# One block for the main loop and the general path, and a wait of TensorE for its own update ahead of each aggregate, in a graph-attention layer with experts

## What is computed

```python
xn = layernorm(x)
h = xn @ W                                    # graph attention, 4 heads of 64
e = leaky_relu(a_src[src] + a_dst[dst], 0.2)  # edges and self loops
p = exp(e - segment_max(e, dst))
gnn = relu(segment_sum(p / segment_sum(p, dst) * h[src], dst) + bias)
q, k, v = split(xn @ w_qkv + b_qkv); k = ln(k); v = ln(v)
mix = gelu((q @ (k.T @ v / N) + xn) @ w1 + b1) @ w2 + b2 + xn
x = x + gnn + mix
xn = layernorm(x) * gamma + beta
logits = xn @ Wr + br                         # 8 experts, the best 2 are taken
out = x + sum over the two of w[e] * (gelu(xn @ W1[e] + b1[e]) @ W2[e] + b2[e])
```

## Time and profile before

| | |
|---|---|
| median of 3 runs | 2322.64 us (2322.01 to 2328.99) |
| profiled execution | 2320.06 us, span 2318.3 us |
| busy in the span | TensorE 1877.7 us (81%), VectorE 1631.3 (70%), ScalarE 939.7 (41%), GpSimd 1705.2 (74%) |
| largest groups | gathers L1385 x1563, 1484.1 us; aggregate L1955 x3136, 903.1 us; L1462 x196, 446.1 us |
| mean granted TensorE clock | 0.887 |
| DMA | 451.34 MB, 195 GB/s |

### The profile page before, as it was taken

How to read it: one execution, slowest core, us unless ns; L and a number is a source line. 1 busy time by engine, 2 the same in 40 slices (tenths; PEclk the granted TensorE clock), 3 DMA queues, 4 the chain that set the end, 5 groups by cost and what they waited for, 6 DMA issues and landing times. The chain is left out here.

```text
span 2318.3 us, 36469 instructions
## 1 busy us (share of the span) xinstructions
PE 1877.7 (81%) x9261; PEld 1440.6 (62%) x9262; DVE 1631.3 (70%) x3677; ACT 939.7 (41%) x1507; POOL 1705.2 (74%) x1860
## 2 busy tenths in 40 slices
PE   8489998777877778768887888888877788888876
PEld 6367776555666656556666666666655566666655
DVE  7578888567887778876766666677656575765664
ACT  5333333345555555544444443343323243433322
POOL 3477777777777777777777777777777777777775
PEclk9789999887887778779999999999888899999988
DMA  8766655966666666677677777687767777787775
GB/s 289 165 193 173 166 159 156 299 186 174 183 182 179 174 183 178 171 200 197 195 198 199 199 198 199 189 223 194 202 198 200 201 197 203 196 213 210 191 214 160
DMA packets 296594, 451.34 MB, mean 195 GB/s; under 512 B 87393, under 2 KB 195028, under 8 KB 295874
## 3 DMA queue, kind: packets, MB, share of 16 engines
q0 software_dynamic: 87360, 242.89, 39.6%
q1 hardware_dynamic: 200028, 195.10, 28.9%
q10 hardware_dynamic: 8998, 10.96, 1.4%
HBM read 390.81 MB, written 62.13 MB: 195 GB/s over the span
## 5 line engine op out<-in xcount | busy, mean ns | idle before, releaser
L1385 POOL DMA_INDIRECT rows_g<-node_table,src_all x1563 | 1484.1, 950 | 485.2 <-issue 478.8
L1955 PE MATMUL psB<-rows_g,pick_e 128*128 128x260 f32 x3136 | 903.1, 452 | 273.0 <-issue 245.2
L1955 PEld LDWEIGHTS psB<-rows_g,pick_e 128*128 128x128 f32 x3136 | 699.6, 229 | 435.1 <-issue 303.4
L1809 ACT ACTIVATE pick_n<-local_row 128x1024 bf16<-128x1024 bf16 x196 | 207.1, 1057 | 788.5 <-PE psA L1944 760.8
L1462 DVE TENSOR_TENSOR rows_g<-rows_g,psD 128x2048 f32<-128x2048 f32 x196 | 446.1, 2276 | 0.0
L1451 DVE TENSOR_TENSOR p_both_e<-rows_g,psD 128x64 f32<-128x64 f32 x196 | 43.4, 221 | 339.3 <-DMA rows_g<-node_table,src_all 330.8
L1437 DVE TENSOR_TENSOR pick_e<-psD,slot_all 128x1024 f32<-128x1024 f32 x196 | 236.0, 1204 | 0.0
L1805 ACT ACTIVATE local_row<-local_row,minus_id 128x1024 bf16<-128x1024 bf16 x196 | 222.6, 1136 | 22.9 <-DMA local_row<-local_dram 14.6
L1990 PE MATMUL psC<-W_f,xnT 128*128 x468 | 222.1, 597 | 6.9 <-DVE hid L1495 6.9
L2040 PEld LDWEIGHTS psD<-W_f,hidT 128*128 128x128 f32 x936 | 178.2, 191 | 73.8 <-issue 55.6
L2040 PE MATMUL psD<-W_f,hidT 128*128 x936 | 221.6, 380 | 0.0
(11 more groups left out here) (327 smaller groups left out, 2279.8 us busy)
## 6 DMA issues: line engine op xcount, KB each, us to landing
local_row<-local_dram SPq DMA_DIRECT2D x196, 256.0 KB
acc<-in_L_ffn_b_dram SPq DMA_DIRECT2D x117, 256.0 KB
rows_g<-node_table,src_all POOLq DMA_INDIRECT x1563
acc<-in_L_ffn_b_dram SPq DMA_DIRECT2D x125, 128.0 KB
xin<-sent_dram SPq DMA_DIRECT2D x117, 128.0 KB
set_dram<-xn SPq DMA_DIRECT2D x117, 128.0 KB
xnT<-xT_dram SPq DMA_DIRECT2D x96, 128.0 KB, 2.6
xT_dram<-xT POOLq DMA_DIRECT2D x49, 128.0 KB, 5.7
```

The lines of the kernel that those rows point to most:

```text
L1385: pool.indirect_dma_start(out=rows_g[:, r, j], out_offset=None, in_=node_table, in_offset=bass.IndirectOffsetOnAxis(ap=src_all[:, g, j:j + ...
L1809: act.activation(pick_n[:], local_row[:, r], ACT.Relu, bias=1.0, scale=-1.0).then_inc(pick_n_ready, 1)
L1955: last = pe.matmul(ps_sum[s % 2][:, 0:AW], pick_e[:, s % SLOTS, j], rows_g[:, s % RING, j, 0:AW], start=(j == 0), stop=(j == EG - 1))
```

## The change

The diff is long because the loop's code moves one level out, into a function `loop_stage` that returns one function per engine. Leaving out white space, this is all of it:

```diff
+NEAR = 6
+    for t in final_at:
+        if final_at[t] == max(final_at.values()):
+            sum_at[t] = max(job_at) + 3
 # first phase
-            raw_at = {15: 0, 17: 1, 30: 2, 32: 3, 36: 4, 43: 5}
-            rows_weighed = {20: (0, 1), 37: (2, 3, 4), 44: (5,), 47: (6,)}
+            raw_at = {15: 0, 17: 1, 26: 2, 30: 3, 36: 4, 42: 5}
+            rows_weighed = {20: (0, 1), 31: (2, 3), 37: (4,), 43: (5,), 47: (6,)}
-                    act.dma_start(W_ext[:, :, 0:D], gnn_W.rearrange("(k p) n -> p k n", p=P)).then_inc(att_in, 16)
                     for w, a in enumerate((att_src, att_dst)):
                         act.dma_start(att_row[:, w * D:(w + 1) * D], a.rearrange("h c -> (h c)").unsqueeze(0)).then_inc(att_row_in, 16)
+                    act.dma_start(W_ext[:, :, 0:D], gnn_W.rearrange("(k p) n -> p k n", p=P)).then_inc(att_in, 16)
+                        dve.tensor_scalar(low[:], first_i[0:1, NG - WINDOWS:NG], float(P * (NT - NEAR)), None, ALU.is_lt).then_inc(beyond_ready, 1)
-                        dve.wait_ge(beyond_ready, 2)
+                        dve.wait_ge(beyond_ready, 3)
+                        dve.tensor_reduce(late_two[:, 2:3], low[:], AX_X, ALU.max).then_inc(beyond_ready, 1)
 # SyncE ahead of the loop
-                        local_rows(0)
+                    for s in range(AHEAD):
+                        local_rows(s)
                         sp.wait_ge(no_rows_set, 1)
-                        sp.dma_start(factor_dram[NT * P:], window[:, WINDOWS - 1]).then_inc(factors_out, 16)
+                    sp.dma_start(factor_dram[NT * P:], window[:, WINDOWS - 1]).then_inc(near_out, 16)
                         sp.wait_ge(parts_ready, 1)
-                        sp.dma_start(factor_dram[0:NT * P].rearrange("(t p) k c -> p t k c", p=P), factor_parts).then_inc(factors_out, 16)
-                        sp.wait_ge(factors_out, 32)
+                    sp.dma_start(factor_rows[:, NT - NEAR:], factor_parts[:, NT - NEAR:]).then_inc(near_out, 16)
+                    sp.wait_ge(near_out, 32)
                         for s in range(STEPS + LAG):
-                            if 1 <= s < NG:
+                        if AHEAD <= s < NG:
                                 local_rows(s)
+                        if s == WINDOWS:
+                            sp.wait_ge(far_out, 16 * len(far_parts))
 # ScalarE ahead of the loop (far_parts: tiles 0 to 14, 15 to 29, 30 to 42)
                         node_picks(0)
+                    act.wait_ge(parts_ready, 1)
+                    for lo, hi in far_parts:
+                        act.dma_start(factor_rows[:, lo:hi], factor_parts[:, lo:hi]).then_inc(far_out, 16)
                         node_picks(1)
 # TensorE, right ahead of sums(s) for every s < NG
+                def marks_seen(s):
+                    if jobs_with(s - 2) and jobs_with(s - 2)[1] != "dense":
+                        pe.wait_ge(h_turned, jobs_with(s - 2)[0] + 1)
+                    elif jobs_with(s + 1) and jobs_with(s + 1)[1] == "block":
+                        pe.wait_ge(x_turned, turn_number[("job", jobs_with(s + 1)[0])] + 1)
+                    elif 3 <= s < PAIRS + 3:
+                        pe.wait_ge(kv_used, s - 2)
+                    elif s + 1 < NG:
+                        pe.wait_ge(picked, s + 2)
 # the last block
+                loop["sync"](sp)        # likewise tensor, scalar, vector: behind the general path
             @block.gpsimd
             def _(pool):
+                loop["gpsimd"](pool)    # ahead of the general path
                 with pool.If(general_value(pool) == 1):
...
+        last_phase.close()
```

More of the change, by code:

```diff
@@ new lines, in up, with turn_h @@
+                            for k in range(KT):
+                                last = pe.matmul(hidden_bank(a)[:, c * P:(c + 1) * P], W1_f[:, a, k, c * P:(c + 1) * P], xdT[:, k],
+                                                 start=(k == 0), stop=(k == KT - 1))
+                    last.then_inc(up_done, 1)
+                def turn_h(n, kind, a, k):
+                    rows, parts = (tile_rows(a), KT) if kind == "mix" else (P, HK)
+                    pe.wait_ge(gelu_done, n + 1)
+                    if n >= 1:
+                        pe.wait_ge(hT_ready, n)
+                    for c in range(parts):
+                        last = pe.transpose(ps_hT[:, c * P:c * P + rows], hid[0:rows, c * P:(c + 1) * P], ident[0:rows, 0:rows])
+                    last.then_inc(h_turned, 1)
@@ new lines, in turn_tile @@
+                def turn_tile(t):
+                    i, rows = route_number(t), tile_rows(t)
+                    pe.wait_ge(xd_ready, i + 1)
+                    if turn_number[("tile", t)] > 0:
+                        pe.wait_ge(xT_taken, turn_number[("tile", t)])
+                    for k in range(KT):
+                        last = pe.transpose(ps_xT[:, (KT + k) * P:(KT + k) * P + rows], xd[0:rows, i % 3, k * P:(k + 1) * P], ident[0:rows, 0:rows])
+                    last.then_inc(x_turned, 1)
@@ new lines, in logits, with count @@
+                def logits(t):
+                    i, rows = route_number(t), tile_rows(t)
+                    pe.wait_ge(xT_taken, turn_number[("tile", t)] + 1)
+                    for k in range(KT):
+                        last = pe.matmul(ps_small[0:rows, logits_at], xdT[:, k, 0:rows], wr_s[:, k], start=(k == 0), stop=(k == KT - 1))
+                    last.then_inc(logits_done, 1)
+                def count(t):
+                    i, rows = route_number(t), tile_rows(t)
+                    pe.wait_ge(both_ready, i + 1)
+                    if i >= 1:
+                        pe.wait_ge(seen_ready, i)
+                    pe.matmul(ps_small[0:rows, count_at], after[0:rows, 0:rows], both[0:rows, i % 2], start=True, stop=False)
+                    pe.matmul(ps_small[0:rows, count_at], ones_all[:, 0:rows], seen[:], start=False, stop=True).then_inc(counted, 1)
@@ new lines, in totals, with kv @@
+                def totals(x):
+                    pe.wait_ge(seen_ready, route_number(SETS[x][1]) + 1)
+                    pe.matmul(ps_small[:, total_at], ones_all[:], seen[:], start=True, stop=True).then_inc(totals_done, 1)
+                def kv(i):
+                    u, rows = i % 2, tile_rows(i)
+                    pe.wait_ge(kvT_in[u], 16 * (i // 2 + 1))
+                    if i >= 2:
+                        pe.wait_ge(kv_biased, i - 1)
+                    for k in range(KT):
+                        last = pe.matmul((ps_up, ps_hT)[u][0:rows, :], xnT[:, u, k, 0:rows], wkv_s[:, k], start=(k == 0), stop=(k == KT - 1))
+                    last.then_inc(kv_done, 1)
@@ L2140, in sem @@
+            return dict(sync=on_sync, gpsimd=on_gpsimd, vector=on_vector, scalar=on_scalar, tensor=on_tensor)
+        with ExitStack() as ph:
+            loop = loop_stage(ph)
+        idle_marks = iter(loop_marks)
         def sem(name):
-            return nc.alloc_semaphore(name)
+            return next(idle_marks)
         stage_met = sem("stage_met")
@@ L3220, in _ @@
                     meet(pe, 5)
+                loop["tensor"](pe)
             @block.scalar
```

1665 lines of the change are left out of this document (813 added, 852 removed).

## The result

| | changed | before | ratio (95%) |
|---|---|---|---|
| median of 8 and 8 runs | 2316.07 us (2314.11 to 2317.67) | 2323.39 us (2322.01 to 2328.99) | 0.9965 (0.9955 to 0.9975) |
| profiled execution | 2317.67 us, span 2315.9 | 2320.06 us, span 2318.3 | |
| the changed kernel again, another chip | 2315.51 us | 2321.35 us | 0.9975 (0.9965 to 0.9986) |

The ratio of 0.9965 is 8.1 us. I had forecast 4.2 us, the second chip shows 5.8, and the two profiled executions are only 2.4 us apart.

What follows compares the result with a forecast made beforehand. GpSimd's issue of indirect DMAs was taken as the bound. First phase +1.1, last sums -0.3 and join -5.0 made -4.2 us, from 2322.64 to 2318.4 us; range 2311.5 to 2325.5.

Steps and rivals of the forecast that it cites:

- The bound: Whole loop: it lasts as long as GpSimd needs to issue 1755 indirect DMAs, about 1.25 us apart.
- Three terms: Span: 95.5 us until GpSimd's first gather, 2207.9 us of issue, 14.9 us from the last DMA's start to the end.
- ring: Slots for gathered rows: gather s stalls GpSimd only if aggregate s-4 is late; slack 7.7 us at aggregate 12.
- Part 1: Last flag check moved to the front, blocks joined: -5.0 us at the end; 5.0 us at the front hidden.
- Part 2: Factor table sent in two pieces: first pick 3.5 us earlier, aggregate 0 ends earlier; worth 0 to the sum.
- this cover: Loop start: the earlier first pick from the split factor table, hiding the other engines' start 5.0 us later.
- Part 3: TensorE's wait ahead of each aggregate: 0.3 us a step (0 to 0.45), hidden in steps 3 to 27; worth 0.
- Part 4: First phase: table loads at tiles 31 and 36 +1.65 us, W_ext behind the attention rows -0.5: first gather +1.1 us.
- Part 5: Last three tiles' sums moved behind the last dense result: store leaves earlier, -0.3 us (-1.0 to +0.5).
- (a): Extra table loads vanish in other waits, some small GpSimd stalls go too: 2314 to 2317 us; chance 0.2.
- (b): The join does less: GpSimd's first instructions late, or the closing block keeps its barrier: 2320 to 2323 us; chance 0.12.
- (c): TensorE's wait stalls GpSimd in steps 3 to 27, slower than before; 2355 us if the clock drops; chance 0.06.

Runs made afterwards that it cites:

- the two kernels with doubled aggregates: Changed kernel with each aggregate's matmuls issued twice, with and without TensorE's wait ahead of each aggregate: 2542.89 us and 2488.18 us; before 2320.91 us.
- the repetition: The changed kernel run again unaltered on another chip: 2315.51 us, 0.9975 of before.
- the old pieces: Score pieces weighed at the old tiles, W_ext loaded ahead of the attention rows; changed kernel with only this undone: 3221.67 us, 1.062, on the slowed chip.

## Why the prediction was right, and where it was not

The forecast of 2318.4 us was 2.3 us above the median and the range held it. Against before, 4.2 us were forecast and 5.8 and 8.1 measured. That the range held says little: 2311.5 to 2325.5 takes in the kernel before as well (2322.64). And part of the nearness is luck, since a term with the wrong sign and a cost put at 0 partly cancel. Step by step:

**The bound: right.** Three terms, and GpSimd's stream among them. Each change that touched neither of its ends nor its ring was worth less than 1 us.

**Part 1, -5.0 us: right.** Undone alone it gives 5.1 us back. The front was mis-sized: I charged the other engines 1.0 us for one more flag load and branch and 4 us for the jump, and VectorE starts 98.51 - 94.89 = 3.6 us later. As the phase ended 0.3 us earlier, the jump and the second load together take 3.9 us, not 5.0. The Trainium skill's 108 ns for a compare-and-branch ("Advanced Engine Details and Errata", "Control Flow Timing") is the figure for the instruction; here it takes less, 44 to 76 ns on four engines. What comes behind a far one is much longer: 3.2 to 3.3 us on SyncE, ScalarE and VectorE in the changed kernel's trace (2.5 to 4.2 over the fourteen traces), 3.4, 3.7 and 3.9 us inside TensorE's own row in three kernels, and 0.4 us on GpSimd.

**Part 2, worth 0: right as a sum, and it is what pays for part 1.** I wrote that without this cover each microsecond of aggregate 0 beyond 0.8 would be one of the total. Undone, it costs 6.4 us, 6.3 of them in one wait at gather 4. The 0.8 was misread: it is the time from aggregate 0's end (129.91) to gather 4 (130.70), and the same 0.79 us stands at each of gathers 4 to 29 of the two kernels with doubled aggregates, where the ring is empty. So it is GpSimd's answer and no room; aggregate 0 had none. The 768 rows landed 3.2 us after their issue, where I had estimated 4.1, and the first pick moved by 114.38 - 119.57 = -5.2 us instead of -3.5; aggregate 0's lower clock took part of that back.

**Part 3, worth 0: nearly.** 10.13 - 9.91 = 0.22 us a step, inside 0 to 0.45, and the ring held. But I said that only an empty ring can slow GpSimd, and the 0.6 to 0.9 us by which the kernel without the wait is faster came with slack in the ring. I also had the ring lose 5 us over 25 steps, because TensorE's step would be longer than GpSimd's. It lost nothing: from an aggregate's end to the gather that takes over its slot it is 7.50 us at every gather from 7 to 21 in the profiled run (8.75 in the repetition), since GpSimd's step grew to 10.13 us too. A likely reason is in the section below. The Trainium skill, "TensorE: Matmul & The Clock Gate", "Step-by-step: what each phase is for", has the weight load pulled ahead of matmuls in flight; no run here shows the lost overlap by itself. I had put 0.2 us a step on it, 39 us if TensorE set the time. With TensorE made the bound the whole wait costs 54.7 us.

**Part 4, +1.1 us: wrong in sign.** The tiles' share was right: two more table loads appear in tiles 31 and 36, and the cast moves from 90.76 to 92.02, +1.26 us. The step that failed is the last one, "these move with the tiles": the engines did not wait for what I named. GpSimd's own closing drain ends last. SyncE, with its landing behind it, reached its drain at 91.83 us before and 92.06 after, so a little later; GpSimd's drain ended at 92.53 before and 92.20 after, the engines meet 0.04 us behind it, and the first gather follows 2.94 to 2.95 us after that meeting. By line, the drain of GpSimd and of SyncE, before and after:

```profile
L506 POOLq DRAIN  x1: 6533/6533/6533, 86.0 to 86.0; - x1
...
L506 SPq DRAIN  x1: 7/7/7, 91.8 to 91.8; - x1
```
```profile
L511 POOLq DRAIN  x1: 4955/4955/4955, 87.2 to 87.2; - x1
...
L511 SPq DRAIN  x1: 7/7/7, 92.1 to 92.1; - x1
```

In the three traces with the old pieces this drain ends 5.97 to 6.05 us after GpSimd's last store, in the eleven with the new ones 4.38 to 4.40 us after it, within 0.01 us of VectorE's. What shortened it is not shown; the last piece also lands sooner now (SyncE's wait ends 2.6 us after its issue instead of 3.6), and whether that has a part in it is open. First gathers with the old pieces: 95.51, 95.83 and 96.00 us; with the new ones, GpSimd's loop first, ten traces between 94.82 and 95.55, mean 95.2. So about -0.6 us, a term mis-signed by 1.7 us.

**Part 5, -0.3 us: worth nothing, and my reading of the end was wrong.** I followed the last store. On the ordinary chips the end hangs on GpSimd: its drain ends 7.43 us after its last DMA's end, and the clearing of semaphores comes behind it. Before, SyncE was through at 2311.20 and GpSimd's drain at 2311.73 us; after, at 2313.2 and 2314.3. The store has 0.5 us of slack before and 1.1 after. On the slowed chip the drain takes the same 7.43 us, but there SyncE's store decides: in the changed kernel's trace GpSimd's drain ends at 3211.0 and SyncE is through at 3226.3 us. What the new order of the sums is worth where the store comes last was not measured: the times of that chip don't tell it.

**The sum.** By the runs: -5.1 (join), -0.6 (first phase), +0.6 (wait), 0 (table, sums) makes -5.1 us, against 5.8 measured on the same chip and 8.1 on the first, whose interval reaches from 5.8 to 10.5. What put 2 us more between the kernels on the first chip isn't known: before's median was 2323.39 there and 2321.35, 2320.91 and 2321.39 on three later chips, the changed kernel's 2316.07 and 2315.51.

**The rivals.** (a) came nearest to the measured time, but not for its reason: the table loads did not vanish, GpSimd's drain got shorter. (b) is out (5.1 us). (c) is out on ordinary chips, where the clock was 0.98 to 1.00 from 130 to 400 us. The changed kernel's 0.99 is below the 1.00 that I had named as a sign of being wrong; the kernels without the wait have 0.98 there and are not slower for it. My chance of 0.06 took all chips for the one of the trace; on the slowed chip the changed kernel is 6.3% slower, though not shown to be so by the wait.

## What to carry to other kernels

Where one engine's instructions follow each other without a pause, look for its first instruction, its last one and what its closing drain takes: here 5.1 us of 5.8 lay behind the last one, and what gated the first one was that engine's own drain as well. A wait that another queue hides has a price, 0.28 us here, and it should be measured with that queue's slack taken away, since on a chip with a slower TensorE it may not be hidden. A gain at one end may need a cover at the other: the join without the split table is worth nothing.

## What the hardware did that I had not expected

- **GpSimd's drain.** It ends 7.43 us after the last indirect DMA's end in all fourteen traces, on both kinds of chip, whether its sequencer had reached it 14 us before that end or 0.2 us before it. Behind the first phase's last store it ends after 4.4 or 6.0 us.
- **The far branch costs by engine.** Over the fourteen traces TensorE 3.3 to 4.1 us, SyncE, ScalarE and VectorE 2.5 to 4.2 us from branch to next instruction, GpSimd 0.4 us. What makes it long, the length of the code skipped or where it lies, was not tried.
- **Two streams of nearly the same period lock.** With the wait, TensorE's step is 10.13 us, and so is GpSimd's: in nearly every step one gather of eight lasts 1.07 us instead of 0.95, always the one that starts while VectorE does L294 (16 of 16 between 130 and 330 us, 18 of 18 in the repetition). Without the wait most of GpSimd's steps are 9.98 to 10.02 us, and only two and four gathers there are long, again all under L294. Over the whole span 41 to 52 gathers last more than 1.03 us in the five ordinary traces with the wait and single aggregates, and 28 to 31 in the three without. From the timeline of the changed kernel's repetition:

```profile
230.48 0.69 DVE L294 TENSOR_TENSOR W_f<-W_f 128x512 f32<-128x512 f32 x1
230.91 1.08 POOL L1400 DMA_INDIRECT rows_g<-node_table,src_all  x1 [0.30 <-issue]
...
240.60 0.69 DVE L294 TENSOR_TENSOR W_f<-W_f 128x512 f32<-128x512 f32 x1
241.05 1.06 POOL L1400 DMA_INDIRECT rows_g<-node_table,src_all  x1 [0.30 <-issue]
```

That 0.12 us in each of some 17 steps is 2 us. The kernel without the wait has two or three steps of 10.4 to 10.5 us there instead, 1.0 to 1.4 us in all, so the difference is of the size of the 0.6 to 0.9 us that the wait costs. That VectorE's operation is what lengthens the gather was not isolated.
- **A slowed TensorE.** On one chip engines that wait for a matmul's update go on about 6 us after its record in the steps looked at, and the kernel before takes 3037 us instead of 2321. The ends of matmuls are modelled in the profile, so it can't be told whether the matmul or its update is late. There the change costs 195 us, 1.0 us a step, over three times the 0.28 that the doubled aggregates gave. That the wait is the cause is likely, as no other part touches TensorE inside the loop, but the kernel without it never ran on that chip, so it stays open.
